# Expert output bias on 128 rows of the matmul, and second layer-norm statistics taken on ScalarE one step later

## What is computed

```python
x = x + attn(layernorm(x))
x = x + moe(layernorm(x))

# attn: q, k = elu(.) + 1; v plain; running sums over the tokens of a sequence
kv   = kv + k[:, None] * v[None, :];  ksum = ksum + k
y    = (q @ kv) / (q . ksum + 1e-6);  attn = y @ W_proj + b_proj

# moe, for each token
routed = softmax(x @ Wr + br) on its two largest experts, renormalized
h      = relu(x @ W1[e] + b1[e]);  out_e = h @ W2[e] + b2[e]
moe    = sum over the two experts of routed[e] * out_e
```

## Time and profile before

| | before |
|---|---|
| median of 3 runs | 402.93 us (401.96 to 403.1) |
| the profiled execution | 401.86 us |
| its span, first to last instruction | 400.1 us |
| mean granted PE clock | 0.894 of 2.4 GHz |
| PE, DVE, POOL, ACT busy | 311.0, 297.5, 280.4, 193.4 us |

### The profile page before, as it was taken

One profiled execution on the slowest core, in us unless ns is written; L12 is line 12 of the kernel. 1 busy time (PEld: TensorE's weight loads), 2 busy tenths in 40 slices (PEclk: granted clock), 3 DMA queues, 4 the chain that ended last, 5 costly groups with the idle time before them and its releaser, 6 DMA issues.

```text
span 400.1 us, 8377 instructions
## 1 busy us (share of the span) xinstructions
PE 311.0 (78%) x2477; PEld 241.8 (60%) x2477; DVE 297.5 (74%) x702; ACT 193.4 (48%) x480; POOL 280.4 (70%) x251
## 2 busy tenths in 40 slices
PE   5899999696979959889841389998999999993000
PEld 4678766464646636666530368887888888882000
DVE  6898998996779898799963777766666667773067
ACT  2788216557223210533312256776677777771072
POOL 3869376899457887887765636878788788787500
PEclk9999999899899987999955569999999999998555
DMA  7970000000000100000110142312423233111198
GB/s 221 346 221 1 2 0 0 2 2 0 2 0 20 35 28 20 27 22 27 41 48 33 47 128 70 81 56 87 115 83 83 83 91 89 43 43 52 46 374 256
DMA packets 23958, 29.26 MB, mean 73 GB/s; under 512 B 3806, under 2 KB 18569, under 8 KB 23916
## 3 DMA queue, kind: packets, MB, share of 16 engines
q1 hardware_dynamic: 18934, 19.02, 15.9%
q0 software_dynamic: 4544, 9.38, 7.3%
q10 hardware_dynamic: 438, 0.33, 0.3%
HBM read 16.04 MB, written 12.67 MB: 72 GB/s over the span
## 4 chain that ended last, share of the span: by engine, by line
PE 32%; DVE 23%; issue 19%; POOL 13%; ACT 9%; DMA 3%; SPq 0%; POOLq 0%; DVEq 0%; ACTq 0%
POOL y_rows L514 9%; PE ps L1191 7%; DVE work L845 4%; PE ps L1190 3%; DVE nd L851 3%; POOL x_rows L479 3%; DVE y_s L862 3%; PE ps L1162 2%; PE ps L1392 2%; ACT xs L610 2%; DVE x L1123 2%; PE ps L1362 2%; PE ps L1393 2%; PE ps L1364 2%; PE ps L1363 2%
## 5 line engine op out<-in xcount | busy, mean ns | idle before, releaser
L514 POOL DMA_INDIRECT y_rows<-kvt,yid x78 | 95.5, 1225 | 30.3 <-issue 21.0
L479 POOL DMA_INDIRECT x_rows<-rows,pos_i x64 | 66.1, 1034 | 30.2 <-issue 17.3
L449 POOL TENSOR_TENSOR kvt<-qk,v 128x1024 f32<-128x1024 f32 x32 | 67.6, 2136 | 24.4 <-PE ps L1195 13.2
L1191 PE MATMUL ps<-kvt,tri 128*128 128x384 f32 (+1 forms) x192 | 70.2, 477 | 12.1 <-DVE work L845 12.1
L676 ACT ACTIVATE wraw<-ps,b1s 128x256 f32<-128x256 f32 x156 | 61.3, 475 | 2.8 <-PE ps L1364 2.5
L1191 PEld LDWEIGHTS ps<-kvt,tri 128*128 128x128 f32 x192 | 37.0, 200 | 33.0 <-issue 16.5
L1071 DVE CAST wraw<-wraw 128x1024 f16<-128x1024 f32 x39 | 27.2, 696 | 34.7 <-ACT wraw L676 33.4
L1075 DVE TENSOR_TENSOR wraw<-wraw 128x1024 f16<-128x1024 f32 x39 | 47.8, 1226 | 1.3
L845 DVE TENSOR_TENSOR work<-ps,qk 128x1152 f32<-128x1152 f32 x32 | 42.2, 1351 | 3.5 <-PE ps L1195 3.2
L1362 PE MATMUL ps<-wraw,w1h 128*128 128x256 f16 x156 | 43.4, 278 | 0.3 <-issue 0.3
L1363 PE MATMUL ps<-wraw,w1h 128*128 128x256 f16 x156 | 43.3, 278 | 0.0
(11 more groups left out here) (211 smaller groups left out, 650.0 us busy)
## 6 DMA issues: line engine op xcount, KB each, us to landing
wraw<-x_rows SPq DMA_DIRECT2D x39, 130.0 KB, 2.6
qk<-y_rows SPq DMA_DIRECT2D x8, 512.0 KB, 6.6
wraw<-in_L_ffn_W_dram SPq DMA_DIRECT2D x1, 2048.0 KB, 11.8
out_dram<-x SPq DMA_DIRECT2D x8, 256.0 KB, 4.5
x<-in_L_attn_x_dram SPq DMA_DIRECT2D x3, 512.0 KB, 7.9
y_rows<-kvt,yid POOLq DMA_INDIRECT x78, 2.5
x_rows<-empty SPq DMA_DIRECT2D x9, 130.0 KB, 3.1
x_rows<-rows,pos_i POOLq DMA_INDIRECT x64, 2.3
```

The costliest lines, as they stand in the source:

```text
L449: nc.gpsimd.tensor_tensor(kvt[:, u % RING, a].rearrange("p (j h i) -> p j h i", j=DH, i=DH), k.unsqueeze(1).broadcast_to([P, DH, H, DH]), ...
L479: nc.gpsimd.indirect_dma_start(out=x_rows, out_offset=bass.IndirectOffsetOnAxis(ap=pos_i[:, c, t:t + 1], axis=0), in_=rows[:, t, :], in_of ...
L514: nc.gpsimd.indirect_dma_start(out=y_rows, in_=ysb[:, n % YG, g], in_offset=None, out_offset=bass.IndirectOffsetOnAxis(ap=yid[:, n, g:g + ...
L1191: nc.tensor.matmul(o, tri[:, :], kv[a][:, cols], start=(a == 0), stop=True)
```

## The change

Two parts that don't touch each other.

The stationary operand of the bias matmul becomes `ones_b` (128x128), and `b2p` gets 128 rows: POOL sets all of it to zero in its preamble (in place of the setting of `ones3`), and SP's transfer of the three pieces fills the first three rows once that is done. The product is the same.

`copy_x2` becomes two ACTIVATEs, one for each tile, which also give the row sums. A new ACT function `statistics(u)`, called in the step after the unit's between `copy_yT(s)` and `copy_x2(s)` (and once behind the loop), scales the sums to minus the mean and takes, tile by tile, the squares of x minus the mean with their row sums; the squares themselves land in `rows`, which is overwritten later. `bn_stats` and `moments_2` leave DVE. POOL's `layer_norm_2` gets one instruction ahead of its two, variance from the sum of squares.

```diff
@@ -114,8 +114,7 @@
         b1T = sb("b1T", [P, E * HC])
         b1s = sb("b1s", [P, E * HC])
         b2hml = sb("b2hml", [E, 3, D], BF16)
-        b2p = sb("b2p", [3, E, D], BF16)
-        ones3 = sb("ones3", [3, P], BF16)
+        b2p = sb("b2p", [P, E, D], BF16)
         ident = sb("ident", [P, P])
         tri = sb("tri", [P, P])
         ones = sb("ones", [P, P])
@@ -143,6 +142,10 @@
 
         st = sb("st", [P, NT, 6])
         lnt = sb("lnt", [P, 7, NT])
+        sums = sb("sums", [P, NT])
+        mean = sb("mean", [P, NT])
+        squares = sb("squares", [P, NT])
+        var = sb("var", [P, NT])
         rstd = sb("rstd", [P, 2, NT])
         shift = sb("shift", [P, 2, NT])
         xT_s = sb("xT_s", [P, 2, T])
@@ -256,8 +259,9 @@
         yT_out = sem("yT_out")
         proj_done = sem("proj_done")
         x2_done = sem("x2_done")
-        bn2_done = sem("bn2_done")
-        stats2_done = sem("stats2_done")
+        mean_done = sem("mean_done")
+        squares_done = sem("squares_done")
+        var_done = sem("var_done")
         rstd2_done = sem("rstd2_done")
         shift2_done = sem("shift2_done")
         xs_done = sem("xs_done")
@@ -342,7 +346,8 @@
             sp.wait_ge(b2_done, 1)
             sp.dma_start(b2_parts.rearrange("r e d -> e r d"), b2hml[:, :, :]).then_inc(b2_in, 16)
             sp.wait_ge(b2_in, 16)
-            sp.dma_start(b2p[:, :, :], b2_parts).then_inc(b2_in, 16)
+            sp.wait_ge(late_done, 16)
+            sp.dma_start(b2p[0:3, :, :], b2_parts).then_inc(b2_in, 16)
 
             regs = [sp.alloc_register(name=f"row{j}") for j in range(XG)]
             for n in range(NBLK):
@@ -403,7 +408,7 @@
             layer_norm_1(1)
             layer_norm_1(2)
             nc.gpsimd.memset(empty[:, :, :], 0.0).then_inc(empty_done, 1)
-            nc.gpsimd.memset(ones3[:], 1.0).then_inc(late_done, 1)
+            nc.gpsimd.memset(b2p[:, :, :], 0.0).then_inc(late_done, 1)
             nc.gpsimd.memset(ones_h[:], 1.0).then_inc(late_done, 1)
             nc.gpsimd.memset(picked[:, 0, :], 0.0).then_inc(late_done, 1)
             nc.gpsimd.iota(ints[:, 0:E], [[1, E]], base=0, channel_multiplier=0).then_inc(late_done, 1)
@@ -464,10 +469,13 @@
 
             def layer_norm_2(g):
                 gt = tiles_of(g)
-                pool.wait_ge(stats2_done, g + 1)
-                nc.gpsimd.tensor_tensor(rstd[:, 1, gt], lnt[:, 4, gt], neghalf[:, gt], ALU.pow).then_inc(rstd2_done, 1)
+                pool.wait_ge(squares_done, G_LAST[g] + 1)
+                nc.gpsimd.tensor_scalar(var[:, gt], squares[:, gt], 1.0 / (D * X_SCALE ** 2), LN_EPS / X_SCALE ** 2, ALU.mult,
+                                        ALU.add).then_inc(var_done, 1)
+                pool.wait_ge(var_done, g + 1)
+                nc.gpsimd.tensor_tensor(rstd[:, 1, gt], var[:, gt], neghalf[:, gt], ALU.pow).then_inc(rstd2_done, 1)
                 pool.wait_ge(rstd2_done, g + 1)
-                nc.gpsimd.tensor_tensor(shift[:, 1, gt], lnt[:, 3, gt], rstd[:, 1, gt], ALU.mult).then_inc(shift2_done, 1)
+                nc.gpsimd.tensor_tensor(shift[:, 1, gt], mean[:, gt], rstd[:, 1, gt], ALU.mult).then_inc(shift2_done, 1)
 
 
             def scatter_x(n):
@@ -596,7 +604,21 @@
 
             def copy_x2(u):
                 act.wait_ge(proj_done, u + 1)
-                nc.scalar.activation(tiles(x, u), ps[:, 7, 0:T].rearrange("p (a d) -> p a d", a=TPU), ACT.Copy).then_inc(x2_done, 1)
+                for a in range(TPU):
+                    t = u * TPU + a
+                    ins = nc.scalar.activation(x[:, t], ps[:, 7, a * P:(a + 1) * P], ACT.Copy, accum_out=sums[:, t:t + 1])
+                ins.then_inc(x2_done, 1)
+
+            def statistics(u):
+
+                act.wait_ge(x2_done, u + 1)
+                nc.scalar.activation(tiles(mean, u), tiles(sums, u), ACT.Copy, scale=-1.0 / D).then_inc(mean_done, 1)
+                act.wait_ge(mean_done, u + 1)
+                for a in range(TPU):
+                    t = u * TPU + a
+                    ins = nc.scalar.activation(rows[:, t, 0:D], x[:, t], ACT.Square, bias=mean[:, t:t + 1],
+                                               accum_out=squares[:, t:t + 1])
+                ins.then_inc(squares_done, 1)
 
             def norm_2(g):
                 act.wait_ge(shift2_done, g + 1)
@@ -636,6 +658,8 @@
                 if s - 3 in ended_by:
                     copy_logits(ended_by[s - 3])
                 copy_yT(s)
+                if s >= 1:
+                    statistics(s - 1)
                 copy_x2(s)
                 if s == 1:
                     act.wait_ge(scale_done, 1)
@@ -645,6 +669,7 @@
                         cast_weights(e)
                 if s - 2 in ended_by:
                     norm_2(ended_by[s - 2])
+            statistics(U - 1)
             for g in (NG - 2, NG - 1):
                 norm_2(g)
                 copy_x2T(g)
@@ -862,18 +887,6 @@
                 nc.vector.tensor_tensor(y_s[:, par].rearrange("p a (h j) -> p a j h", j=DH), ndp[:, :, 0:DH, :],
                                         rd[:, par].unsqueeze(2).broadcast_to([P, TPU, DH, H]), ALU.mult).then_inc(y_done, 1)
 
-            def statistics(u):
-                dve.wait_ge(x2_done, u + 1)
-                for a in range(TPU):
-                    t = u * TPU + a
-                    nc.vector.bn_stats(st[:, t, :], x[:, t, :]).then_inc(bn2_done, 1)
-
-            def moments_2(g):
-                gt = tiles_of(g)
-                dve.wait_ge(bn2_done, gt.stop)
-                moments(gt.start, gt.stop, -1.0)
-                variance(gt.start, gt.stop, 1.0 / X_SCALE ** 2).then_inc(stats2_done, 1)
-
             def split_low(g):
                 for u in range(G_U0[g], G_LAST[g] + 1):
                     dve.wait_ge(xh_done, u + 1)
@@ -933,8 +946,6 @@
                     dve.wait_ge(wall_done, 1)
                     link(nc.vector.tensor_copy(sc[:, 4:7], ps[:, 6, T + P:T + P + 3]))
                 reduce(s, 1)
-                if s >= 1:
-                    statistics(s - 1)
                 quotient(s)
                 if s == 1:
                     scales()
@@ -942,8 +953,6 @@
                     bias_scales()
                 if s - 5 in ended_by:
                     positions(ended_by[s - 5])
-                if s - 1 in ended_by:
-                    moments_2(ended_by[s - 1])
                 if s - 3 in ended_by:
                     split_low(ended_by[s - 3])
                 if s - 4 in ended_by:
@@ -1034,8 +1043,6 @@
                 link(nc.vector.tensor_tensor(outside[:, 0], outside[:, 0], outside[:, 1], ALU.max))
                 link(nc.vector.tensor_tensor(aside[:, :, :], outside[:, 0], spare[:, :, :], ALU.mult))
 
-            statistics(U - 1)
-            moments_2(NG - 1)
             choose(FIRST)
             positions(FIRST)
             counts(0)
@@ -1381,7 +1388,7 @@
                 if n == SPREAD + 2:
                     pe.wait_ge(table_done, 4)
                 both = ps[:, 6 + n % 2, 0:GPB * D].rearrange("p (g d) -> p g d", g=GPB)
-                nc.tensor.matmul(both, ones3[:, :], b2p[:, bass.ds(e, 1), :].broadcast_to([3, GPB, D]), start=True, stop=False)
+                nc.tensor.matmul(both, ones_b[:, :], b2p[:, bass.ds(e, 1), :].broadcast_to([P, GPB, D]), start=True, stop=False)
                 outs = [ps[:, 6 + n % 2, g * D:(g + 1) * D] for g in range(GPB)]
                 high = [(w2[:, bass.ds(e, 1), c, 0].rearrange("p a d -> p (a d)")) for c in range(HC)]
                 low = [(w2[:, bass.ds(e, 1), c, 1].rearrange("p a d -> p (a d)")) for c in range(HC)]
```

## The result

On the chip of these runs the kernel before takes 402.44 us (median of 4 runs, 400.38 to 403.1) and the change 397.85 us (4 runs, 395.72 to 397.97): a ratio of 0.9873, 95% interval 0.9844 to 0.9902, so 3.9 to 6.3 us faster. The profiled execution takes 397.97 us (span 396.2) beside 401.86 (span 400.1). The sign, the place and the rough size are as predicted; of the 7.4 us of the bias part some 5.7 arrive.

A forecast was written before the change was run, and what follows sets the result against it. PE was taken to pace the experts' stage, with POOL's backlog ending it, and ACT to pace six late loop steps. -7.4 - 3.6 + 4.2 + 0.3 = -6.5 us on the median 402.93 gave 396.4 us, range 392.0 to 403.9.

The forecast's parts named there:

- the 7.4 us of the bias part: Experts' stage: 0.20 x 39 blocks = 7.8 us off PE, less 0.4 for PE's earlier wait for x rows.
- The cause of the gap: PE's bias matmul: a weight load of few rows doesn't run beside the matmul before it; 0.42 us where 0.22 is normal.
- A block would take 2.99 instead of 3.19.: Experts' stage: each PE block gets 0.20 us shorter once the bias matmul has 128 rows.
- POOL's backlog stays at some twelve scatters and the end moves with PE.: End of experts' stage: DVE's subtract holds POOL 0.2 us less a block, a scatter pair still goes out per block.
- the third rival: Experts' stage: DVE's cast L1071 holds POOL too, its backlog grows, up to all 7.4 us is lost; chance 0.08.
- 7.6 us of `bn_stats` are worth nothing: Attention loop: the two `bn_stats` stand where DVE waits for ACT's denominator anyway, so removing them gains nothing.
- ACT: +4.2: Attention loop: added ACT work costs 0.7 us in each of six steps (2, 4, 5, 6, 8, 11) where ACT is late.
- DVE waits some 4 us more: Attention loop, sign in the profile after: DVE's wait for ACT's denominator grows by some 4 us.
- Moments -3.6, POOL +0.3: Loop: moments leaving DVE save 4 x 0.9 us (steps 6, 9, 11, 13); POOL's extra instruction costs 0.3 at its end.
- The rows as no cause: Rival on the bias matmul: the gap has another cause, blocks stay at 3.19, 403.8 us; chance 0.10.
- Dear row sums: Rival on ACT in the loop: the change loses from 0.37 us a row sum; at 0.48 it gives 407.4; chance 0.07.
- POOL doesn't follow: Rival, experts' stage: POOL sends less than a pair a block; 400.1 us at half the loss, 403.8 at all; chance 0.08.

The follow-up runs named there:

- bias64: Kernel before with ones and pieces of the bias matmul in 64 rows, statistics left on DVE; 417.22 us against 417.75, ratio 0.9992.
- static3: Kernel before with expert 0's weights and bias for every block, bias still in 3 rows; 417.34 us against 420.07, ratio 0.9932.
- static128: Kernel before with expert 0 for every block and the bias over 128 rows, statistics on DVE; 414.63 us against 420.07, ratio 0.9867.
- bias_only: Kernel before with only the bias matmul over 128 rows, statistics left on DVE, on a slow chip; 416.16 us against 417.75, ratio 0.9978.
- bias_only_2: Kernel before with only the bias matmul over 128 rows, run again on a chip of 402 us; 395.76 us against 401.74, ratio 0.9860.
- no_subtract: Kernel before with the 128-row bias matmul and DVE's subtract of the low halves replaced by a cast; 390.33 us against 402.06, ratio 0.9680.
- no_row_sums: The whole change without ACT's four row sums a step, constants in their place; 394.03 us against the kernel before's 401.74, ratio 0.9819.

## Why the prediction was right, and where not

**The cause of the gap.** Right. bias64 shows that 64 rows are no better than 3, and static3 that the address from a register has no part in it. The rule of the Trainium skill ("TensorE: Matmul & The Clock Gate", section "LDWEIGHTS (loading the stationary operand)"), that few rows load as slowly as many, remains true of the instruction (the weight load takes 0.091 us with 3 rows and 0.099 with 128) and misses the start, as the prediction held. The loads themselves, in the kernel before and in the change:

```profile
303.07 0.09 PEld L1384 LDWEIGHTS ps<-b2p,ones 3*128 3x128 bf16 x1 [0.21 <-issue]
```

```profile
301.42 0.10 PEld L1391 LDWEIGHTS ps<-b2p,ones_b 128*128 128x128 bf16 x1
```

The load of 3 rows starts 0.20 behind the start of the matmul ahead of it (302.87), the one of 128 rows with it (301.42). The zeroing of `b2p` cost nothing, as predicted: it takes 0.96 us, POOL's wait ahead of the last power falls from 3.05 to 2.18, and that power starts at 25.45 before and 25.48 after.

**"A block would take 2.99 instead of 3.19."** It takes 3.03 on average (from the copy of y at 285.10 to that at 354.75 it is 23 blocks). The 0.04, in 36 blocks 1.5 us, is the small gap among the matmuls of the second layer (42 more of them than before, 2.5 us by the count); static128 shows that these gaps come, most of them, with the address instructions (35 beside the 176 of bias_only and the 171 of the whole change, all on slow chips). That the 0.42 around the bias matmul used to give PE's stream the time for them is my reading, and wasn't tried by itself.

**"POOL's backlog stays at some twelve scatters and the end moves with PE."** The mechanism is right, and its size was too large. Count the blocks from 0: from block 13 to block 31 the first scatter of a block follows ACT's copy of that block by 13.1 to 13.8 us in the kernel before, 9.7 to 10.4 in the change and 11.4 to 11.6 in bias_only_2. Over these 18 blocks the scatters take 57.4, 54.5 and 54.6 us, and the copies 57.4, 54.4 and 54.4: one pair in one block, at PE's pace, though POOL never pauses. What ties POOL to PE is how DVE holds it. Timeline of the change:

```profile
293.43 0.69 DVE L1078 CAST wraw<-wraw 128x1024 f16<-128x1024 f32 x1 [0.70 <-ACT wraw L701]
293.53 1.42 POOL L522 DMA_INDIRECT y_rows<-kvt,yid  x1 [0.30 <-issue]
...
294.16 1.22 DVE L1082 TENSOR_TENSOR wraw<-wraw 128x1024 f16<-128x1024 f32 x1
...
295.26 0.95 POOL L522 DMA_INDIRECT y_rows<-kvt,yid  x1 [0.30 <-issue]
```

The scatter starts inside the cast and ends 0.83 behind it (293.53 + 1.42 = 294.95; 293.43 + 0.69 = 294.12). In the kernel before, 28 of the 33 scatters longer than 1.1 us start inside the subtract and end 0.82 to 0.84 behind that; in the change 22 of 33 start inside the cast and 10 inside the subtract, with the same 0.82 to 0.84. So the third rival's condition came true, the cast holds POOL as well, and so did what the prediction set against it: held there, a scatter is free 0.43 us before the subtract ends, and the pair is kept. no_subtract shows that the subtract keeps the tie: with a cast in its place a pair takes 2.87 us while a block takes 3.04, and the lag shrinks from 11.1 us at block 13 to 8.1 at block 31.

Why then 5.7 and 5.9 us from the first to the last scatter (in the change and in bias_only_2), and not 7.4? The term that was mis-sized is the block: 3.03 for 2.99 leaves 0.16 us of the 0.20. The first 13 pairs bring 2.4 and 2.6 us, the next 18 bring 2.9 in both, and from block 31 to the last scatter it is 0.4: the last 9 to 11 scatters are sent behind DVE's last subtract, 0.96 us each, and there is nothing to shorten in them. The prediction took 0.20 for each of the 39 blocks. PE's wait for x rows, priced at 0.4, is longer than that: the gap between the copies of blocks 11 and 12 is 5.15 us before, 7.25 in the change and 5.89 in bias_only_2. POOL sends on meanwhile, a pair every 3.0 us, so this shortens its backlog and costs the end nothing. The scatters that start behind the last copy of y are 11 before, 9 in the change and 10 in bias_only_2, not the same number as forecast.

**"7.6 us of `bn_stats` are worth nothing", "ACT: +4.2".** Right in both. Over the six late steps DVE's wait is 12.3 us before and 18.9 in the change: 6.6 more, 2.8 of it for the `bn_stats` that no longer fill the 0.46 of plain latency, and 3.8 for ACT's lateness, against the 4.2 forecast. The row sum was mis-sized (0.19 for 0.1), but part of it is hidden, so that its 2.4 us became 2.8 (no_row_sums). That leaves 1.0 for the mean, the squares and the second copy, which were put at 1.8: the sum is nearly right because two misses cancel in part. What was wrong is the sign to look for: "DVE waits some 4 us more" left out the latency of all sixteen steps; it waits 10.7 us more.

**"Moments -3.6, POOL +0.3", so the statistics part +0.9.** Not settled. Measured 0.0 us (-1.0 to +0.8) on a chip of 402 us and +2.3 (1.0 to 3.5) on one of 418: +0.9 lies between the two, just outside either interval. The difference of the whole change and the bias part, +0.5, is known to some 1.7 us either way. No run takes the moments alone. One profiled execution can't settle it: where POOL and DVE happen to meet, the product with the reciprocal (`y_s`) takes 0.62 or 2.47 us, and the first y scatter comes at 240.6 to 246.3 us in the seven traces whose loop is that of the kernel before (mean 243.2), and at 241.7 to 245.4 in the five with the change's loop (mean 243.9). The 1.9 us between the two traces of the result are within that.

**The rivals.** The rows as no cause: refuted. Dear row sums: 0.19 is far below the 0.37 needed. "POOL doesn't follow": its condition came true, its loss did not, for the reason given above. What none had: a chip on which PE's gain is slack and the change slower.

## What to carry to other kernels

Give a matmul of a few rows all 128, with zeros in the rest, where its weight load must run beside the matmul ahead of it: 0.20 us each here, of which 0.16 were left in the block, at no price that a run shows but memory. An engine that never pauses can still keep another's pace, if each round of that other holds it once: before counting what PE saves, look whether the lag between the two stays the same over many blocks, and in which blocks nothing is held, since there nothing is gained. And price what does the holding; taking 0.5 us of DVE's work out of a block brought as much again as the bias part did. And with two engines that hold each other, don't read a part's price of one or two us from one trace: run the part alone, and on more than one chip.

## What the runs showed of the hardware

- A weight load of 3 or of 64 rows starts 0.20 us behind the start of the matmul ahead of it, one of 128 rows together with it; so the starts of the matmuls are 0.20 and 0.22 us apart with 3 and 64 rows and 0.11 and 0.11 with 128, with the same moving operand from a register address.
- A row sum on ACT is a separate instruction of 0.186 to 0.193 us behind each ACTIVATE.
- A POOL scatter (0.96 us by itself) that starts inside DVE's f32 to f16 cast (0.69 us) or its two-operand subtract (1.23 us), and lasts over 1.1 us, ends 0.82 to 0.86 us behind the end of that instruction: so do all 118 such scatters in the traces of the kernel before, the change, bias_only_2 and no_subtract. Eleven more that start within 0.04 us of a cast's start are not held; there the cast takes 0.73 to 0.77 us.
- Of PE's small gaps in the second layer (0.13 us between starts instead of 0.055), 176 and 171 stand in two slow traces with addresses from a register, and 35 in one with constant addresses.
- Two of the four chips of the experiments take 15 to 18 us longer for the same kernel. Traces of other kernels show most or all of it in the experts' stage: 13 to 16 us more in its first six blocks, then blocks of 3.5 to 3.6 us, with ACT waiting 1.2 us ahead of its copy of y for something the profile doesn't name. The cause was not found.
